# Moving two steps on VectorE and one on ScalarE within a pair of tiles: a gather and projection stage on Trainium2

## What is computed

```python
proj = einsum('bchw,oc->bohw', x, Wc) + bc
flows = einsum('bchw,koc->kbohw', x, Woff) + boff      # 4 heads, (x, y) each
weights = softmax(einsum('bchw,kc->bkhw', x, Wwt) + bwt, axis=1)
vgrid = base + flows                                   # where each head looks
feats = bilinear_sample_zeros(proj, vgrid)             # 4 corners of each place
out = einsum('kbohw,bkhw->bohw', feats, weights)
x = x + out
```

## Time and profile before

| | us |
|---|---|
| median of 3 runs | 708.02 |
| lowest and highest | 707.51, 708.26 |
| the profiled execution, its own time | 709.86 |
| its span, first to last instruction | 708.1 |

### The profile page before, as it was taken

The page is one execution under the profiler, slowest core; times in us unless marked ns, Lnnn a source line. Parts: engine busy times, 40 slices in busy tenths (PEclk is TensorE's granted clock), DMA queues, the critical chain, the costliest instruction groups (busy, mean ns, idle before and its releaser), DMA issues.

```text
span 708.1 us, 10473 instructions
## 1 busy us (share of the span) xinstructions
PE 605.9 (86%) x2889; PEld 479.4 (68%) x2889; DVE 549.0 (78%) x1316; ACT 362.1 (51%) x892; POOL 364.0 (51%) x385
## 2 busy tenths in 40 slices
PE   1999799999997888598959977997889889699787
PEld 0444475778886777486848866886777767587666
DVE  6999774579998775696849766985698759698567
ACT  0298885788995442352543536363544535355221
POOL 0030593235554475466556656666565665666630
PEclk9999999999999566699879989998989979989899
DMA  9900001137767799799989999999999999999992
GB/s 358 373 23 0 0 1 47 44 89 214 213 212 238 238 370 334 283 357 401 350 326 340 400 359 367 367 371 351 393 358 360 385 383 326 381 379 357 375 347 60
DMA packets 77366, 197.04 MB, mean 278 GB/s; under 512 B 7337, under 2 KB 36812, under 8 KB 77196
## 3 DMA queue, kind: packets, MB, share of 16 engines
q0 software_dynamic: 43488, 154.55, 59.2%
q1 hardware_dynamic: 33836, 42.03, 17.0%
HBM read 168.05 MB, written 28.51 MB: 278 GB/s over the span
## 4 chain that ended last, share of the span: by engine, by line
DVE 32%; another core or an unknown queue 14%; issue 13%; PE 7%; POOL 0%; DVEq 0%; ACT 0%
DVE ps L1166 20%; PE ps L1536 3%; DVE ps L1163 2%; DVE xs L1180 2%; PE ps L1486 2%; DVE wq L1166 1%; DVE wvs L1166 1%; DVE wvs L1173 1%; PE ps L1562 1%; DVE wq L1173 1%; PE ps L1563 0%; DVE weights L1116 0%; PE ps L1595 0%; DVE pos L1079 0%
## 5 line engine op out<-in xcount | busy, mean ns | idle before, releaser
L956 POOL DMA_INDIRECT v<-table,index x252 | 236.2, 937 | 152.8 <-issue 64.0
L1536 PE MATMUL ps<-v 128*128 128x256 f32 x786 | 215.7, 422 | 49.5 <-issue 24.0
L1536 PEld LDWEIGHTS ps<-v 128*128 128x128 f32 x786 | 163.5, 213 | 87.1 <-issue 38.9
L1166 DVE SCALAR_TENSOR_TENSOR ps<-v,weights,ps 128x256 f32<-128x256 f32 x489 | 214.5, 482 | 3.4 <-DVE ps L1166 1.5
L1313 ACT ACTIVATE v<-ident,weights 128x128 f32<-128x128 f32 x464 | 139.3, 388 | 13.9 <-remote 11.2
L1326 ACT COPY pick_mask<-ps 128x512 f32<-128x512 f32 x18 | 10.5, 585 | 137.5 <-remote 115.6
L1405 PE MATMUL ps<-wq,s_ring 128*128 128x256 f32 x288 | 68.1, 380 | 1.0 <-ACT ps L1249 0.9
L943 POOL TENSOR_TENSOR xs<-xs,v 128x512 f32<-128x512 f32 x36 | 45.1, 1274 | 46.0 <-DVE v L1013 46.0
L1326 ACT COPY sample<-ps 128x512 f32<-128x512 f32 x17 | 9.9, 584 | 104.3 <-remote 57.5
L1180 DVE TENSOR_TENSOR xs<-ps,xs 128x512 f32<-128x512 f32 x35 | 23.9, 682 | 46.9 <-remote 46.9
L1405 PEld LDWEIGHTS ps<-wq,s_ring 128*128 128x128 f32 x288 | 53.9, 191 | 9.4 <-issue 2.9
(11 more groups left out here) (174 smaller groups left out, 955.2 us busy)
## 6 DMA issues: line engine op xcount, KB each, us to landing
table<-stage SPq DMA_DIRECT2D x72, 256.0 KB, 3.2
xs<-in_x_dram SPq DMA_DIRECT2D x11, 768.0 KB, 11.1
out_dram<-xs SPq DMA_DIRECT2D x28, 256.0 KB
v<-table,index POOLq DMA_INDIRECT x252
early<-const_syn POOLq DMA_DIRECT2D x18, 192.0 KB, 3.8
ana<-const_ana SPq DMA_DIRECT2D x1, 2304.0 KB, 20.0
out_dram<-xs SPq DMA_DIRECT2D x7, 238.0 KB
stage<-table,index POOLq DMA_INDIRECT x36
```

Source lines behind the costliest of these rows:

```text
L956: nc.gpsimd.indirect_dma_start(places[a], None, table, bass.IndirectOffsetOnAxis(ap=index[:, t, k:k + 1], axis=0)) \
L1166: V.scalar_tensor_tensor(to, corner, weight, ps[:, DVE_SUM, i * C:(i + 1) * C], ALU.mult, ALU.add).then_inc(added, 1)
L1536: m = T.matmul(ps[:, PE_SUM[i], 0:C], diag[2 * u + i][n], places[a][:, q * C:(q + 1) * C], start=n == 0, stop=n == len(mine) - 1)
```

## The change

On DVE, the result of a projection is added to x in the middle of a pair, after the join of tile 2p-1, and it is that of pair p-4, instead of that of pair p-3 at the end of the pair; pair 34 does both its own late one and one at its end, so that the last pair is as before. `locate` and `soften` go from the beginning of the pair to the same middle. On ACT, `tents` goes behind `diags`.

```diff
 for p in range(PAIRS):
-    for g in range(UP_FRONT, len(SIZES)):
-        if max(FIRST[g] // 2 - 4, 0) == p:
-            locate(g)
-            soften(g)
     for a in TURNS[2 * p]:
         add(*a)
     if p >= 1:
         join(2 * p - 1)
     if p == LAST:
         result(p - 3)
+    elif p >= 4:
+        result(p - 4)
+    for g in range(UP_FRONT, len(SIZES)):
+        if max(FIRST[g] // 2 - 4, 0) == p:
+            locate(g)
+            soften(g)
     for g in range(UP_FRONT, len(SIZES)):
         if FIRST[g] // 2 - 3 == p:
             weigh(g)
...
     join(2 * p)
     if p == LAST:
         result(p - 2)
-    elif p >= 3:
+    elif p == LAST - 1:
         result(p - 3)
```

```diff
 for p in range(PAIRS):
     if ROLLED <= p + 1 < NO_FLOWS:
         fetch(p + 1)
+    if p + 1 < PAIRS:
+        for t in range(2 * p + 2, 2 * p + 4):
+            diags(t)
     for g in range(UP_FRONT, len(SIZES)):
         if max(FIRST[g] // 2 - 4, 0) == p:
             tents(g)
-    if p + 1 < PAIRS:
-        for t in range(2 * p + 2, 2 * p + 4):
-            diags(t)
     if p >= 1:
         keep(p - 1)
```

## The result

| | before | after |
|---|---|---|
| median, us | 708.14 (4 runs) | 702.39 (4 runs) |
| lowest and highest | 707.51, 708.93 | 701.35, 703.65 |
| profiled execution | 709.86, span 708.1 | 702.67, span 700.8 |

The ratio is 0.9919 with a 95% interval of 0.9899 to 0.9939, so 4.3 to 7.2 us are gone. The forecast was 701.0, with a range of 696 to 709.

A forecast was written before the change was run, and what follows sets the result against it. Nearly every engine was taken as near full in the gathers' stage, with DVE's steps worth only what they give back to gathers; 4.1 + 2.9 = 7.0 us off the 708.02 median gave 701.0 us, range 696 to 709.

The forecast's parts named there:

- Bound: Gathers' stage, some 250 to 690 us: DMA share 0.98, so DVE steps count only by what they return to gathers.
- Holds last until POOL pauses: Stretches where TensorE's signals reach others late, ending 1.6 to 1.8 us after POOL's last issue of a run; cause unknown.
- First group: First locate in the loop, near 290 us: adds done during the hold free POOL's slots; gain 4.1 us, the DMA's figure.
- Second group: Second locate in the loop, near 365 us: POOL resumes 3.9 us earlier, but DMA idles only 2.9; gain 2.9 us.
- The three others: Remaining locate groups in the loop: POOL loses little to DVE's adds there; counted 0, with 2.8 us kept for the range.
- Tail: After the last hold, ending at 678.61 us: nine adds done ahead could save up to 3.5 us; counted 0.
- The result's new place: Result of pair p-4 behind join 2p-1: never waits by itself, the wait becomes the join's; cost 0.
- My own sign of failure: Forecast wrong if waits at joins total the same 80 us with POOL's last issue still near 683 us.
- ScalarE's order: Diagonals ahead of distances in five pairs: undoes a cost of moving locate; by itself 0.
- Given back: Rival, chance 0.23: gathers set the time and the head start is lost; gain 0 to 2 us, 706 to 708.
- The second half gets too long: Rival, chance 0.15: between joins 2p-1 and 2p DVE takes 5.0 us against PE's 4.3; kernel slower, 711 to 713.6.

The follow-up runs named there:

- f1: Kernel before with only the result step moved half a pair later, on a chip with holds: 706.63 us against 707.30, ratio 0.9991.
- f2: Kernel before with locate, soften and ScalarE's order moved, result left at the pair's end, on a chip with holds: 701.92 us against 707.30, ratio 0.9918.
- e3: Full change but ScalarE still does distances ahead of diagonals, on a chip without holds: 665.57 us against 666.18 for the kernel before, ratio 0.9987.

## Why the prediction was right, and where it was not

*Bound.* "Nearly everything is near full, and a step of DVE is worth only what it gives back to the gathers": shown. DVE's waits fell by 15 us of 97 and the time by 6 to 7. The gain is near what the DMA engines got back in the two holes, 6.4 us (7.0 us of missing share before, 0.6 after), and f1 and f2 show that the 47 us at `result` are not where it comes from.

*Holds last until POOL pauses.* Nearly always. Of the 25 waits of DVE of 3 us and more in the two traces, 24 end 1.6 to 2.6 us after POOL's last issue; the one at 334.59 in the kernel before ended while POOL went on issuing. The 1.6 to 1.8 us of the prediction are those of the shorter runs (1.7 to 1.9 after eight gathers in a row). After eleven or twelve it was 2.3 to 2.6 us, in the kernel after (283.86 + 0.94 to 287.15; 355.84 + 0.94 to 359.38) and in the kernel before alike (2.35 us before 678.61). What makes a hold stays open. That it belongs to the chip, its state or what else runs on it, and not to the kernel alone, is shown by the same kernel running 666 us without them.

*First group, 4.1 us.* Measured 3.7 with the late start taken out (3.1 by the clock of the span), between POOL's 3.4 and the DMA's 4.1. The start that I had worked out for tile 8, 292.6, is near the measured 292.84, but in part by luck. I had POOL issue the two `stage` gathers and then pause. In fact it paused earlier and longer, 3.06 us before 287.87 where it had been 1.74, and then issued eight gathers in a row. The wait of 5.04 us for DVE's adds is gone, as forecast; how much of it is kept was not followed right.

*Second group, 2.9 us.* Measured 2.7, by the same route: 5.3 us won at the `stage` gather (0.30 instead of 5.60), 0.3 at the next, and 3.0 lost just before, in a pause of 3.31 us at 360.09 that the kernel before hadn't there. The forecast put 3.9 on POOL and cut it to the DMA's 2.9. With a head start that swings by 2 us and more, an agreement within 0.4 us at both groups is luck in part; the waits that went are not.

*The three others, counted 0.* Measured -0.2 up to the last gather, again a difference of two points of a swinging quantity. Their `stage` waits in the kernel before, 1.25 us at most, were as small as counted; the f1 run shows that in another execution a 5 us wait can fall on one of them.

*Tail, counted 0 with 3.5 as its bound.* Measured 1.6. The last hold met DVE at a join, as thought, but then the result that pair 34 keeps at its end waited 2.85 us for its projection, which I had left out.

*Sum.* 7.0 forecast; 7.2 to 7.3 between the profiled executions, 5.75 (4.3 to 7.2) between the medians. In the former 0.4 too much at the first group, 0.2 each at the second and in the others, and the 0.6 of the late start nearly cancel the 1.6 of the tail. So the mechanism was right and the closeness of the number is partly luck.

*The result's new place.* Cost 0, gain 0: f1 agrees, to within 0.4%. "The wait becomes the join's" was half of it: 25.7 us went to the last add of a tile, which waits until PE has turned the sums whose buffer it fills. I hadn't followed that wait.

*My own sign of failure,* joins and adds waiting "the same 80 us with POOL's last issue still near 683", came true in its first half (79.5 us) and not its second. The first half was no sign of anything.

*ScalarE's order.* No effect to be seen without holds (e3, 0.9987). With holds it was not tried apart from `locate`. PE's wait for diagonals, 5.89 us, is gone from the list, but so is the join's that came with it. Open.

*Rivals.* "Given back" is what happens without holds: at 406 GB/s the memory path sets the time and the ratio is 1.0002. The figure of some 358 GB/s between memory and a core (the Trainium skill, "SBUF — State Buffer", section "A bandwidth-pool intuition that's wrong") is not a limit that this core kept to: it moved 406 GB/s for 350 us by the same row, and 363 to 365 on the chips with holds. "The second half gets too long" didn't occur: PE waited 2.3 us for joins in all. Nor did POOL's issuing suffer from the adds beside it: a gather's median issue time went from 937 to 941 ns.

## What to carry to other kernels

Ask of a wait not how long it is but what is queued behind it on its engine and who needs that. Put a step whose input comes late, and whose output is wanted late, behind the work that frees other engines' buffers. And time such a change on more than one chip: this one is worth 0.8% where signals come late, and nothing that can be measured where they don't. Lay two traces side by side at more than two points before giving a gain to a place: here the head start swung by some 4 us between them.

## What the runs showed of the hardware

The same kernel took 706 to 708 us on some chips and 666 on another. The difference is in the gathers' stage, 363 to 365 GB/s against 406. Where it is slow, TensorE's signals are seen late: the flows of the earlier trace rows end at 282.2 and wake DVE at 289.68, 7.5 us later. In the two traces 24 of 25 long waits of DVE end 1.6 to 2.6 us after POOL stops issuing gathers, the later the longer the run before it. Where it is fast, ACT follows PE within 0.04 us. And with no more than four gathers of 512 KB under way the rate was 329 GB/s instead of 406.
